# Second layer of an expert network: weights in two blocks of 128 columns instead of one half of 256

## The reference, cut to what matters

```python
x = x + xattn(layernorm(x), ctx, ...)                 # x: 4 x 1024 x 512
grouped = layernorm(x).reshape(B, g, t, d)            # B = 4, groups of t = 32 tokens
perm = one token per group, expert and set (argmax)   # 32 experts x 4 sets
dispatched = einsum('bgtd,bgtes->bgesd', grouped, perm)
inner = relu(einsum('bgesd,desf->bgesf', dispatched, f1) + bias)   # layer one
intermediate = einsum('bgesf,esfd->bgesd', inner, f2)              # layer two
out = einsum('bgesd,bgtes->bgtd', intermediate, perm)              # combine
x = x + out
```

## Time and profile before

| | |
|---|---|
| median of 3 runs | 1151.2 us (1145.01 to 1152.91) |
| profiled execution, its time | 1149.39 us |
| its span, first to last instruction | 1147.4 us |
| PE busy, share of the span | 1101.9 us, 96% |
| DVE, ACT, POOL busy | 881.1, 598.0, 508.8 us |
| granted TensorE clock, mean | 0.989 |
| layer two and combine (first `make` to the end) | 1034.1 to 1147.4 us |

### The profile page before, as it was taken

One profiled execution on the slowest core, in us unless ns is written; L12 is line 12 of the kernel. 1 busy time (PEld: TensorE's weight loads), 2 busy tenths in 40 slices (PEclk: granted clock), 3 DMA queues, 4 the chain that ended last, 5 costly groups with the idle time before them and its releaser, 6 DMA issues.

```text
span 1147.4 us, 28430 instructions
## 1 busy us (share of the span) xinstructions
PE 1101.9 (96%) x10904; PEld 768.3 (67%) x10904; DVE 881.1 (77%) x2229; ACT 598.0 (52%) x1100; POOL 508.8 (44%) x722
## 2 busy tenths in 40 slices
PE   7999999999999999999999999999999998989896
PEld 6787888888566555655565556555688886875453
DVE  6756776665688888888888888886599886758676
ACT  4322222223566666666666666667444435546684
POOL 1000000010677788777778887776566540000234
PEclk9999999999999999999999999999999999988899
DMA  8978897769855545666545566622599986661867
GB/s 290 325 259 283 300 337 257 246 233 272 207 119 117 116 115 133 149 148 141 114 115 117 113 144 148 149 69 75 175 310 303 314 274 190 193 186 49 283 192 231
DMA packets 167620, 223.40 MB, mean 195 GB/s; under 512 B 10688, under 2 KB 95168, under 8 KB 167488
## 3 DMA queue, kind: packets, MB, share of 16 engines
q1 hardware_dynamic: 167488, 221.62, 65.7%
HBM read 143.69 MB, written 77.63 MB: 193 GB/s over the span
## 4 chain that ended last, share of the span: by engine, by line
PE 85%; DMA 7%; DVE 2%; issue 2%; ACT 2%; POOL 1%; SPq 1%; POOLq 0%; DVEq 0%; ACTq 0%
PE p_bank L1716 14%; PE p_bank L1736 13%; PE p_bank L1755 12%; PE p_bank L1798 7%; PE p_bank L1799 7%; PE p_bank L1800 7%; PE p_bank L1774 7%; PE p_bank L863 3%; DMA kept_f<-in_f 3%; PE p_bank L390 2%; PE p_bank L353 2%; PE p_bank L351 2%; PE p_bank L352 2%; PE p_bank L875 2%; PE p_bank L839 1%
## 5 line engine op out<-in xcount | busy, mean ns | idle before, releaser
L1625 ACT ACTIVATE p_t<-p_bank 128x512 f32<-128x512 f32 (+1 forms) x608 | 303.9, 582 | 122.4 <-PE p_bank L1736 122.0
L1486 DVE CUSTOM_DVE_ANT_0 tried<-p_bank,ban 128x512 bf16<-128x512 f32 (+3 forms) x512 | 228.3, 485 | 53.4 <-PE p_bank L1716 53.2
L1716 PE MATMUL p_bank<-k_stack,q_stack 96*128 96x512 f32 (+3 forms) x768 | 233.4, 364 | 1.4 <-ACT p_t L1625 0.9
L1736 PE MATMUL p_bank<-q_stack,k_stack 97*128 97x512 f32 (+3 forms) x768 | 218.0, 354 | 1.5 <-DMA q_stack<-m_row 1.1
L1716 PEld LDWEIGHTS p_bank<-k_stack,q_stack 96*128 96x128 f32 x768 | 135.7, 189 | 71.7 <-issue 33.5
L1489 DVE TENSOR_REDUCE mx_ab<-p_bank 128x1 f32<-128x512 f32 x256 | 163.8, 684 | 0.0
L1755 PE MATMUL p_bank<-p_t,v_tile 128*32 128x512 f32 (+3 forms) x1536 | 160.3, 492 | 0.6 <-POOL p_t L1358 0.6
L1736 PEld LDWEIGHTS p_bank<-q_stack,k_stack 97*128 97x128 f32 x768 | 132.7, 189 | 33.6 <-DVE mx_e L1486 9.8
L1373 POOL TENSOR_TENSOR p_sum<-p_sum,p_t 128x512 f32<-128x512 f32 x120 | 150.4, 1282 | 0.0
L1362 POOL TENSOR_SCALAR_AFFINE_SELECT p_t<-p_t 128x128 f32<-128x128 f32 (+2 forms) x288 | 100.9, 361 | 87.0 <-ACT p_t L1625 82.9
L607 POOL TENSOR_TENSOR kept_o_sum<-kept_o_sum,kept_x_in 128x512 f32<-128x512 f32 x22 | 28.1, 1287 | 171.8 <-ACT kept_o_sum L697 165.0
(11 more groups left out here) (136 smaller groups left out, 2088.6 us busy)
## 6 DMA issues: line engine op xcount, KB each, us to landing
q_stack<-q_hi SPq DMA_DIRECT2D x64, 256.0 KB, 6.5
k_stack<-k_hi SPq DMA_DIRECT2D x30, 512.0 KB, 9.8
x_in<-in_x SPq DMA_DIRECT2D x8, 1024.0 KB, 9.8
x_t<-in_x_t SPq DMA_DIRECT2D x8, 1024.0 KB, 9.0
k_hi<-k_hi_s SPq DMA_DIRECT2D x8, 1024.0 KB, 5.9
k_lo<-k_lo_s SPq DMA_DIRECT2D x8, 1024.0 KB, 7.8
v_rows<-v_out SPq DMA_DIRECT2D x8, 1024.0 KB, 7.7
q_hi<-q_hi_s SPq DMA_DIRECT2D x8, 1024.0 KB, 4.3
```

What stands on the lines that cost most here:

```text
L1486: dve.tensor_tensor_reduce(scrap, got, ban0[:] if i == 0 else ban[:, CH - w:CH], 1.0, -3e38, ALU.add, ALU.max, to[:, col:col + 1]).then_in ...
L1625: act.activation(pt[:, k % SLOTS_P, u * m:(u + 1) * m, 0:w], bank[:, RINGS["score", n][0], 0:m * w].rearrange("p (m w) -> p m w", m=m), AC ...
L1716: pe.matmul(bank[:, to, 0:w], qs[it % SLOTS][0:R, i * P // CH, h, i * P % CH:i * P % CH + P], ks[it % SLOTS][0:R, h, t0:t0 + w], start=Tru ...
L1736: mm = pe.matmul(bank[:, to, h % m * w:(h % m + 1) * w], ks[slot][0:R + 1, h, j * P:(j + 1) * P], qs[slot][0:R + 1, sh, h, CH - w:CH], sta ...
```

## The change

Layer two works on blocks of 128 columns. There are four of them; two are held at a time, in two buffers of 2 MB (`f2_blocks`, in the same room as before). `HELD` names the blocks held in four phases of two units: (0,2), (1,2), (1,3), (0,3). From one phase to the next one buffer changes (`CHANGED`). `batch(u)` gives the units the batches 0,1,2,3,0,1,2,3, so that batches 0 and 1 meet (0,2) and (1,3), batches 2 and 3 meet (1,2) and (0,3). So 6 MB are loaded late, at three places, where it was 4 MB at one. The blocks lie contiguous in memory, so that a partition's part of a transfer is one run of 2 KB instead of runs of 1 KB.

A unit's two blocks need not be neighbours among the 512 columns. So rows of `x` are loaded, and sums stored, in two transfers of 128 KB (runs of 512 B) where it was one of 256 KB (runs of 1 KB). The counts of the semaphores double.

```diff
+    BLOCK = D // 4
+    f2 = nc.alloc_sbuf_tensor_at("f2_blocks", [P, 2, E4, BLOCK], F32, offset=kept.at["x0"])
+    PIECE = E4 // 4
+    HELD = ((0, 2), (1, 2), (1, 3), (0, 3))
+    CHANGED = (None, 0, 1, 0)
+    def batch(u):
+        return u % 2 + u // 2 % 2 * 2
+    def block(x, v, h):
+        return x[batch(v // WS) * WS + v % WS][:, :, HELD[v // WS // 2][h]]
...
-        def load_late(i):
-            sp.wait_ge(made, (B - 1) * PAIRS + 2 * i + 2)
+        def load_late(t, mp):
+            buf = CHANGED[t]
+            sp.wait_ge(made, (2 * t - 1) * PAIRS + 2 * mp + 2)
             for q in range(2):
-                es = slice(q * PIECE // 2, (q + 1) * PIECE // 2)
-                sp.dma_start(f2[i][:, es], f2_src[i][:, es, DH:D]).then_inc(f2_late[i], 16)
+                es = slice((2 * mp + q) * PIECE // 2, (2 * mp + q + 1) * PIECE // 2)
+                sp.dma_start(f2[:, buf, es], f2_src[HELD[t][buf]][:, es]).then_inc(f2_late[mp], 16)
         def load_x(v):
...
-            sp.dma_start(x2_at(v), x2_src[v // WS // B, v % (B * WS)]).then_inc(x_in[v % XR], 16)
+            for h in range(2):
+                sp.dma_start(half(x2_at(v), h), block(x2_src, v, h)).then_inc(x_in[v % XR], 16)
...
-            sp.dma_start(o_dst[v // WS // B, v % (B * WS)], o_at(v)).then_inc(stored[v % SR], 16)
+            for h in range(2):
+                sp.dma_start(block(o_dst, v, h), half(o_at(v), h)).then_inc(stored[v % SR], 16)
...
+        for mp in range(4):
+            load_late(1, mp)
         for v in range(LAST):
             store(v)
...
-            if WS <= v + 1 < WS + len(f2):
-                load_late(v + 1 - WS)
+            for t in range(2, len(HELD)):
+                if v == (2 * t - 3) * WS - 1:
+                    load_late(t, 0)
+                    load_late(t, 1)
+                elif v == (2 * t - 3) * WS + 1:
+                    load_late(t, 2)
+                    load_late(t, 3)
...
-            b, h, mp, qp = u % B, u // B, pair // 2, pair % 2
+            b, mp, qp = batch(u), pair // 2, pair % 2
             n = u * PAIRS + pair
-            if b == 0 and h == 0:
-                landed(pe, f"f2_{mp}")
-            elif b == 0:
-                pe.wait_ge(f2_late[mp], 32)
+            if u == 0:
+                for buf in range(2):
+                    landed(pe, f"f2_{buf * 2 + mp // 2}", mp % 2 * 2 + 2)
+            elif u % 2 == 0:
+                pe.wait_ge(f2_late[mp], 32 * (u // 2))
...
-                        mm = pe.matmul(bank[c * GT:(c + 1) * GT, n % RING * 2 + q % 2, i * DH:(i + 1) * DH],
-                                       inner[part, e, b * GT:(b + 1) * GT], f2[e // PIECE][part, e % PIECE],
+                        mm = pe.matmul(bank[c * GT:(c + 1) * GT, n % RING * 2 + q % 2, i * DH:(i + 1) * DH].rearrange("p (h d) -> p h d", h=2),
+                                       inner[part, e, b * GT:(b + 1) * GT], f2[part, :, e],
```

More of the change, by code:

```diff
@@ L472, in experts_of @@
     paced = [sem(f"paced{i}") for i in range(PACED)]
-    f2_late = [sem(f"f2_late{i}") for i in range(len(f2))]
+    f2_late = [sem(f"f2_late{i}") for i in range(4)]
     PIECES = (("rows2", 8), ("f1_2a", 4), ("rows3a", 4), ("f1_2b", 4), ("rows3b", 4), ("f1_3a", 4), ("f2_0", 4), ("f1_3b", 4),
@@ L503, in experts_of, with half @@
     f1_src = a.f1.rearrange("(k p) (e f) -> k p (e f)", p=P, f=F)
-    x2_src = m.x2.rearrange("(w n p) (h d) -> h w p n d", n=UT, p=P, d=DH)
-    o_dst = a.out.rearrange("b s d -> (b s) d").rearrange("(w n p) (h d) -> h w p n d", n=UT, p=P, d=DH)
+    x2_src = m.x2.rearrange("(w n p) (q d) -> w p n q d", n=UT, p=P, d=BLOCK)
+    o_dst = a.out.rearrange("b s d -> (b s) d").rearrange("(w n p) (q d) -> w p n q d", n=UT, p=P, d=BLOCK)
     p_src = m.pick.rearrange("i e t -> e i t")
-    f2_src = a.f2.rearrange("p (i e) d -> i p e d", e=PIECE)
+    f2_src = a.f2.rearrange("p q e d -> q p e d")
+    def half(rows, h):
+        return rows[:, :, h * BLOCK:(h + 1) * BLOCK]
     def sync(sp):
@@ L533, in load_f2 @@
             for q in range(4):
-                es = slice(q * PIECE // 4, (q + 1) * PIECE // 4)
-                issue(f"f2_{i}", q, f2[i][:, es], f2_src[i][:, es, 0:DH])
-        def load_late(i):
-            sp.wait_ge(made, (B - 1) * PAIRS + 2 * i + 2)
+                es = slice((i % 2 * 4 + q) * PIECE // 2, (i % 2 * 4 + q + 1) * PIECE // 2)
+                issue(f"f2_{i}", q, f2[:, i // 2, es], f2_src[HELD[0][i // 2]][:, es])
+        def load_late(t, mp):
+            buf = CHANGED[t]
+            sp.wait_ge(made, (2 * t - 1) * PAIRS + 2 * mp + 2)
             for q in range(2):
-                es = slice(q * PIECE // 2, (q + 1) * PIECE // 2)
-                sp.dma_start(f2[i][:, es], f2_src[i][:, es, DH:D]).then_inc(f2_late[i], 16)
+                es = slice((2 * mp + q) * PIECE // 2, (2 * mp + q + 1) * PIECE // 2)
+                sp.dma_start(f2[:, buf, es], f2_src[HELD[t][buf]][:, es]).then_inc(f2_late[mp], 16)
         def load_x(v):
@@ L550, in load_last_x @@
             for v in range(LAST, NV):
-                sp.dma_start(x2_at(v), x2_src[v // WS // B, v % (B * WS)]).then_inc(x_late[v - LAST], 16)
+                for h in range(2):
+                    sp.dma_start(half(x2_at(v), h), block(x2_src, v, h)).then_inc(x_late[v - LAST], 16)
         def store(v):
             wait_added(sp, v)
-            sp.dma_start(o_dst[v // WS // B, v % (B * WS)], o_at(v)).then_inc(stored[v % SR], 16)
+            for h in range(2):
+                sp.dma_start(block(o_dst, v, h), half(o_at(v), h)).then_inc(stored[v % SR], 16)
         def store_last(part):
@@ L560, in store_last @@
                 sp.wait_ge(added_last[part], v - LAST + 1)
-                sp.dma_start(o_dst[v // WS // B, v % (B * WS)][:, :, cols], o_at(v)[:, :, cols]).then_inc(stored_last, 16)
+                sp.dma_start(block(o_dst, v, part), o_at(v)[:, :, cols]).then_inc(stored_last, 16)
         sp.wait_ge(raw_in, 32)
@@ L597, in sync @@
         for i in range(SR):
-            sp.wait_ge(stored[i], 16 * len(range(i, LAST, SR)))
+            sp.wait_ge(stored[i], 32 * len(range(i, LAST, SR)))
         sp.wait_ge(stored_last, 16 * PARTS * WS)
@@ L1905, in build @@
         keep.wide = put("wide", [P, NE * NGR])
-        keep.x2_in = put("x2_in", [P, 3, 4, P])
-        keep.o_sum = put("o_sum", [P, 4, 4, P])
+        keep.x2_in = put("x2_in", [P, 3, 2, 2 * P])
+        keep.o_sum = put("o_sum", [P, 4, 2, 2 * P])
         project_attend_route(nc, a, m, keep)
```

20 lines of the change are left out of this document (8 added, 12 removed).

## The result

The changed kernel takes 1153.4 us in the median of 19 runs, the kernel before 1148.6 us in 19 runs on the same chip. The ratio is 1.0039, with a 95% interval of 1.0025 to 1.0052, so it is slower by 4.5 us (2.9 to 6.0); one thousandth is 1.15 us here. In a second series it was 1.0050 (1.0033 to 1.0067). The forecast was 1147.5 us, 3.7 us faster. The time lies inside the range, but the change goes the other way. The profiled execution took 1155.4 us, its span is 1153.4.

What follows compares the result with a forecast made beforehand. It took PE and DVE as near the limit in undisturbed loops, with SP's queue bounding the end. Terms -8.0 + 0 + 1.0 + 1.0 + 2.3 = -3.7 us gave 1147.5 us from the median 1151.2; range 1141 to 1156.

Steps and rivals of the forecast that it cites:

- The wait for 4 MB goes: Loop that makes unit 4: PE's wait for late weights disappears, 19.0 us becoming 11.0, worth -8.0 us.
- First change of a block: Ahead of unit 2: weight pieces land in time or behind PE's wait for ACT; cost 0, up to 0.7 us uncovered.
- Second and third change: Ahead of units 4 and 6: weights land slightly late behind doubled row transfers; +1.0 us each, range 0 to 1.9.
- third rival: SP's queue becomes the bound: gain gone at 0.56 us per transfer; at 0.65 us, +5.7 us, 1156.9 us; chance 13%.
- second rival: The wait only moves: pieces ahead of units 4 and 6 land after 7.2 us, clock falls; +3.1, 1154.3 us; chance 15%.
- Undisturbed loops: Loops without a weight change: 16 SP transfers take 7.6 of 11.0 us, so both halves fit; cost 0.
- The end: Last sums, loads and stores on SP's queue: more issues, less a shorter landing; +2.3 us, ends 0.2 and 3.2.
- The operand in two runs: Pair matmuls reading 2 x 128 columns 16 KB apart: taken as 0, at most 1.3 us.

Runs made afterwards that it cites:

- GpSimd's queue: The changed kernel with the late weights of the second and third change issued from GpSimd's queue instead of SP's: ratio 1.0012 to the kernel before.
- the kernels with none, 3 and 6 MB: The changed kernel with one transfer per load and store of rows, and that much late weight: ratios 0.9960, 0.9987 and 1.0019 to the kernel before.
- the four kernels with one wait per pair: Changed kernel, unit 0's pairs waiting once for weights: alone 1.0018; with neighbouring blocks and early weights 0.9987; neighbours and GpSimd's queue 1.0005; GpSimd's queue 1.0023.
- the one with 448 matmuls and as many weight loads more: The changed kernel with each sum four tiles of one block, one row transfer per sum, twice as many combine matmuls: ratio 1.0097 to the kernel before.

## Why the prediction was wrong, by its own steps

**"The wait for 4 MB goes: -8.0 us."** Mis-sized: it measured -3.9 us (-1.5 to -6.3). The step took one loop of the trace against its undisturbed neighbours as the whole gain. The two loops do get 6.1 us shorter, but part of what the wait had hidden comes back as PE idle without a releaser (0.71, 0.33 and 0.44 us above), and the rest of the gap is within the uncertainty of the ratio and of a single profile. With -3.9 in this term the forecast of -3.7 us becomes +0.4.

**First change of a block: 0.** Right. PE has no wait for weights ahead of unit 2; ACT is what it waits for, 2.26 us (1.96 before).

**Second and third change: +1.0 each.** This is the step that failed most. The 6 MB cost the changed kernel 9.4 us, and by the profile the loops around the two changes lie 4.8 and 5.7 us above twice 10.5 us. The median landing was right, the start of the issues was wrong. At the second change, sums 2 and 3 held the queue 5.6 us, not 4.5. Sums 4 and 5, between the two groups of weights, took 6.1 us, not 3.8, because the queue stood 2.1 us waiting for a sum; less that wait they took 4.0, as priced. At the third change it is backlog: the first piece starts 8.5 us after its loop (1099.96 less 1091.44), where the forecast carried over 6.1 us (1071.2 less 1065.07). From 1078.18 to 1108.11 us the queue issues 47 transfers and waits for nothing, 0.64 us each. I priced the queue at medians, 0.43 us for a store with its gap and 0.52 us for a load, 7.6 us of the 11 of a loop. But every few transfers one takes 1 us and more without waiting for anyone (five of those 47, 1.15 to 1.90 us; the maximum of 1.80 us in the earlier trace rows is such a one), and the mean with the gap is 0.59 to 0.65 us. A loop without weights then fills the queue (16 transfers from 1084.21 to 1094.62 us, 0.65 us each, no wait among them), and eight transfers of weights push it behind. The kernel before shows the same mean: from 1084 to 1130 us its queue waits 25.4 us, which leaves 20.6 us for 33 transfers, 0.62 each. Adding up the timeline, less its waits, would have told it. So the **third rival**, with 13%, named one mechanism that is there, and its sign (issues over 0.56 us on average in those loops) is met. At 0.59 to 0.62 us its formula gives +2.1 to +3.9 us against the 4.5 measured; that this is near is in part luck, since it, too, counted on the whole 8.0 us. The **second rival** (+3.1 us, landing after 7.2 us) is near in number as well, but not in its mechanism: the pieces landed after 4.1 us at the median and 5.7 at most. Its fall of the clock behind the waits did come: in the kernel before, the 64 matmuls of 3.09 us behind the 3.92 us ran at 0.50, in the changed one those behind the 1.66 and the 2.18 us at 0.63 and 0.50. Taking the queue's load away (GpSimd's queue, single transfers) gave back 2 to 4 us of the 9.4.

**What the rest is.** With on-time weights PE still stands, without a releaser, while the DMA engines are full. Stretches that end with such an idle and begin 0.5 us ahead of it, first the kernel with GpSimd's queue:

```profile
1072.97:1075.55 2.58, 0.51 (x24) 0.02 (x4) 2.43 (x3) 1.19 (x2) 0.33 (x1) 1.00 1.07 347
1098.24:1101.03 2.79, 0.50 (x19) 0.02 (x2) 0.00 (x0) 1.20 (x2) 0.34 (x1) 0.94 1.11 337
```

then the kernel before without late weights:

```profile
1073.55:1074.76 1.21, 0.50 (x12) 0.02 (x4) 1.21 (x3) 1.21 (x2) 0.10 (x1) 1.00 0.56 173
1079.14:1079.97 0.83, 0.50 (x25) 0.02 (x3) 0.83 (x2) 0.83 (x2) 0.00 (x0) 1.00 0.15 49
```

PE is busy 0.5 us in each and idle for the rest: 2.1 and 2.3 us with the engines full (share above 1), 0.7 and 0.3 us with them half or nearly empty. That the bytes of weights lengthen these idles is shown by the kernels with none, 3 and 6 MB. No run settled what PE waits for in them; that it is its own instructions is my inference from times (last section).

**Undisturbed loops: 0.** The number is right (10.5 us in the kernel without late weights), its reason wrong: the second halves do not fit with room to spare, they fill the queue. The loads suffered, too: DVE waited 6.26 us for rows at two sums, which only happened to lie in loops that PE had delayed.

**The end: +2.3.** Mis-sized, +3.7 us in the profile. Of its terms, the eight last loads' issue is right (4.14 us instead of 2.13). The landing saved is 2.7 us (2.4 instead of 5.1), where I took 0.9. Against that, the last loads start 1.3 us after the start of the last combine where they started 2.1 us before it. That is +3.4 us where I had +1.1, and it is the queue's backlog again. The last addition thus comes 2.6 us later after that combine (7.5 instead of 4.9 us), and the last stores, which used to be issued while it waited, now all stand behind it: +1.1.

At the end a half lands in 2.4 us; a whole takes 5.1 us in the kernel before and 5.3 in the changed one with single transfers. To gather the rows in single transfers is still worth it beside late weights (1.0019 for single transfers, 1.0050 for doubled ones on the same chip), through the issue and not the landing (from 1065 to 1120 us SP's queue waits for others 21 us with single transfers, 5.4 us with doubled ones); without late weights it made no difference (0.9960 and 0.9957).

**The operand in two runs: 0.** Right: four pairs take 3.36 us, as in the earlier trace rows.

**Not in the prediction:** the start of layer two, +2.7 us. In the four kernels with one wait per pair the first combine starts 21.5 to 22.5 us after the first pair, in the changed kernel 24.7 (1056.75 less 1032.03). But the ratios don't agree on a gain, and the kernel without late weights had doubled waits, the same idle of 1.00 us, and 22.5 us, at a clock of 1.00 from 1036 to 1042 us (0.53 in the changed kernel). So it hangs on whether the clock falls after that idle, and what decides that is open.

## What to carry to other kernels

Price a queue that is to take more transfers by its timeline over a loop, less its waits, and divided by the transfers, not by the median of one issue (here 0.62 us, against 0.43 and 0.52); how long it waits for others now is its whole slack. A stall seen in a trace is the most that its removal can win; leaving out the work behind it (here a few lines without late weights) measures what it is worth, and it was half (3.9 of 8.0 us). Before cutting transfers in two, look at what shares their queue: the same doubling cost nothing without late weights and 4.8 us beside them. Loading in smaller pieces at more places paid in no version here (0.9987 to 1.0097), against half as many bytes again (6 MB for 4).

## What was not expected of the hardware

- A transfer of 128 KB holds SP's queue as long as one of 256 KB (medians of 0.47 to 0.50 us for the loads of rows in the changed kernel, 0.47 to 0.49 in the one before), but lands in 2.4 us instead of 5.1 to 5.3 at the end.
- The length of an idle alone didn't tell whether the granted clock fell. It was low after 2.18 us in the changed kernel (128 matmuls in 5.25 us instead of 3.36, clock 0.50) and full after 2.62 us at its end (64 matmuls in 2.07 us, clock 1.00); after 1.00 us it was 0.53 in the changed kernel (1036 to 1042 us) and 1.00 in the one without late weights.
- PE stands 0.2 to 2.3 us at a time (once 3.3) for nothing that the profile names, in nearly every kernel here and most in the one with 448 matmuls and as many weight loads more (12.4 us). In the kernel with halves and no late weights the loops have no such idle. The profile counts a queue "instruction" on the same 16 DMA engines, in the changed kernel 85 packets, 1.39 MB, thus 16 KB each. In the quarter of a microsecond from 1098.50 us, the kernel with GpSimd's queue has this one:

```profile
q8 instruction: 1, 0.02, 24.1%
```

It ends at 1099.65 us, and PE's idle of 2.29 us ends at 1101.03 us, 1.4 us later. So it is nearly everywhere. In layer two of the 17 traces, 64 idles of 0.3 us and more have no releaser, and 63 of them end 1.2 to 1.6 us after the end of such a packet (one 2.3 us), among them the 1.00 us at the start of the changed kernel. The 77 idles with a releaser end 0.1 to 9.0 us after one. From these times alone I infer that PE waits for its instructions and that these packets bring them, beside weights and rows. No run shows it, since none changed these packets by themselves.
